# Linear attention: token turns moved from TensorE through DRAM squares to VectorE, normalisation moved to GpSimd

## What is computed

```python
# layer 0: shifted-window attention, windows of 7 x 7, 4 heads of 32
x = x + L0_conv(_gn(x), w_qkv, pos_emb, w_out, b_out)
# layer 1: tokens t = (16, 3136, 128)
t = t + L1_attn(_ln_t(t), W, b)
t = t + L1_ffn(_ln_t(t), W, V, gamma, beta)

def _ln_t(v, eps=1e-5):            # normalise each token over its channels
    m = mean(v, -1); s = var(v, -1)
    return (v - m) / sqrt(s + eps)

def L1_attn(x, W, b):              # linear attention, causal
    q, k, v = split(x @ W.T + b)
    q = elu(q) + 1; k = elu(k) + 1
    kv_cum = cumsum(k outer v); k_cum = cumsum(k)
    return (q @ kv_cum) / (q . k_cum + 1e-6)

def L1_ffn(x, W, V, gamma, beta):  # batch norm of x @ W.T over all tokens, then
    y_t = sigmoid(wx_t + y_(t-1) @ V.T)   # a recurrence over the tokens
```

## Time and profile before

| | us |
|---|---|
| median of 3 runs | 1781.64 (1780.31 to 1782.01) |
| the profiled execution | 1784.76 |
| its span | 1782.8 |

### The profile page before, as it was taken

The page is one execution under the profiler, slowest core; times in us unless marked ns, Lnnn a source line. Parts: engine busy times, 40 slices in busy tenths (PEclk is TensorE's granted clock), DMA queues, the critical chain, the costliest instruction groups (busy, mean ns, idle before and its releaser), DMA issues.

```text
span 1782.8 us, 58142 instructions
## 1 busy us (share of the span) xinstructions
PE 1749.7 (98%) x19648; PEld 1587.7 (89%) x19648; DVE 1509.8 (85%) x4546; ACT 1269.8 (71%) x3387; POOL 1073.7 (60%) x1202
## 2 busy tenths in 40 slices
PE   7999999999999999989999999999999999989997
PEld 6888888888888888879999999999999999989997
DVE  7889888888888888778888888888888888868787
ACT  5877778887887788856666666666666666657776
POOL 6887888888888888843333333333333333368874
PEclk9999999999999999999999999999999999999999
DMA  5333343433333332313334434343434443457774
GB/s 167 105 103 104 104 110 99 109 107 102 110 103 104 106 106 70 83 43 70 73 67 68 70 68 70 68 67 68 70 68 70 68 68 70 86 178 277 291 278 176
DMA packets 361816, 188.30 MB, mean 106 GB/s; under 512 B 221760, under 2 KB 348720, under 8 KB 356656
## 3 DMA queue, kind: packets, MB, share of 16 engines
q1 hardware_dynamic: 360368, 183.40, 41.0%
q10 hardware_dynamic: 1152, 1.13, 0.2%
HBM read 106.58 MB, written 77.87 MB: 103 GB/s over the span
## 4 chain that ended last, share of the span: by engine, by line
PE 52%; issue 28%; POOL 17%; DVE 1%; DMA 1%; POOLq 0%; ACT 0%; ACTq 0%; SPq 0%; DVEq 0%
POOL la_rstd L1025 12%; PE k_psum L349 7%; PE k_psum L299 6%; PE k_psum L292 6%; PE k_psum L1488 6%; PE k_psum L317 6%; PE k_psum L333 6%; PE k_psum L365 5%; PE k_psum L1478 5%; PE k_psum L283 5%; POOL la_spread L1019 3%; POOL la_tn L1030 2%; DMA wa_group<-in_group 0%; POOLq L42 0%; DMA t<-la_tn 0%
## 5 line engine op out<-in xcount | busy, mean ns | idle before, releaser
L1019 POOL TENSOR_SCALAR la_spread<-la_mv 128x4 f32<-128x4 f32 (+1 forms) x203 | 46.2, 228 | 476.1 <-DVE la_mv L1130 476.0
L618 POOL TENSOR_TENSOR wa_prob<-wa_prob,wa_peak 128x784 f32<-128x784 f32 x128 | 195.0, 1523 | 116.8 <-DVE wa_peak L484 116.8
L966 ACT ACTIVATE la_ve<-k_psum 128x256 f32<-128x256 f32 x196 | 75.6, 386 | 231.9 <-PE k_psum L847 231.9
L1025 POOL TENSOR_TENSOR la_rstd<-la_spread,k_exponent 128x4 f32<-128x4 f32 (+1 forms) x203 | 207.8, 1024 | 17.2 <-POOL la_spread L1019 0.4
L625 POOL TENSOR_TENSOR wa_prob<-wa_prob,wa_inv 128x784 f32<-128x784 f32 x128 | 195.2, 1525 | 11.3 <-DVE wa_inv L445 11.3
L835 PE MATMUL k_psum<-la_uT,la_wt 128*128 128x256 f32 x784 | 201.9, 380 | 0.0
L1085 DVE SCALAR_TENSOR_TENSOR la_fqk<-k_psum,la_raised 128x512 f32<-128x512 f32 x196 | 135.4, 691 | 72.8 <-ACT la_raised L958 72.6
L1562 ACT ACTIVATE sc_y<-k_psum,sc_cols 128x128 f32<-128x128 f32 x414 | 152.3, 368 | 51.9 <-PE k_psum L1488 8.8
L476 DVE TENSOR_TENSOR wa_prob<-k_psum,wa_bias 128x784 f32<-128x784 f32 x128 | 124.9, 976 | 66.2 <-PE k_psum L317 66.1
L1488 PE MATMUL k_psum<-sc_y,sc_vT 128*128 128x128 f32 x824 | 171.0, 289 | 0.0
L958 ACT ACTIVATE la_raised<-k_psum,la_minus_one 128x512 f32<-128x512 f32 x196 | 134.8, 688 | 43.9 <-PE k_psum L835 43.7
(11 more groups left out here) (137 smaller groups left out, 5205.3 us busy)
## 6 DMA issues: line engine op xcount, KB each, us to landing
la_xc<-x SPq DMA_DIRECT2D x196, 128.0 KB, 3.0
wa_xT<-in_x_cm SPq DMA_DIRECT2D x124, 196.0 KB, 3.3
sc_tb<-t SPq DMA_DIRECT2D x17, 1320.0 KB, 8.3
out<-sc_ob SPq DMA_DIRECT2D x17, 1280.0 KB, 5.4
wa_xw<-in_x_tok SPq DMA_DIRECT2D x64, 224.0 KB, 2.7
wa_xw<-in_x_tok SPq DMA_DIRECT2D x64, 168.0 KB, 2.3
x<-wa_y SPq DMA_DIRECT2D x64, 168.0 KB, 2.8
x<-wa_y SPq DMA_DIRECT2D x48, 224.0 KB, 2.9
```

Of the source, the lines that this page charges most:

```text
L618: nc.gpsimd.tensor_tensor(s, s, peak[:, k % S, :].unsqueeze(2).broadcast_to([128, PAIRS * HEADS, WIN]), ALU.subtract).then_inc(lowered, 1)
L1025: nc.gpsimd.tensor_tensor(rstd[:, n % S, used], spread[:, used], exponent[:, used], ALU.pow).then_inc(rooted, 1)
```

## The change

Tokens are no longer turned by TensorE. GpSimd normalises unit n (now as x * rstd + shift with shift = 1 - mean * rstd, which contains the added 1) into `u`, four pieces of 32 channels apart. When both units of a pair are there, SyncE stores the pair to a new DRAM tensor `squares` (`store_normed`, 128 partitions of 2 KB). One step later SyncE waits for that store to land and loads the pair again with four DMAs (`load_squares`), each of which puts one quarter of the channels on 32 partitions. Then VectorE turns 32 x 32 squares in `us` into `uT` with one instruction per unit (`turn_tokens`). `turned_out` on ScalarE and `turn_tokens` on TensorE are gone. Token loads run eight steps ahead (`xc` has 12 buffers), statistics and normalisation seven and six steps ahead; `steps` begin at -8, and JOIN is NU - 7. To make room, `uT` has three buffers and `raised` two.

The diff, cut to its core (signatures, semaphore lists and places where only XS becomes XC are left out):

```diff
@@ -70,0 +71 @@
+    squares = nc.dram_tensor("squares", (B * T // 512, 128, QUADS, 4 * SQ), F32, kind="Internal").ap()
...
@@ -206 +207 @@
-        JOIN = NU - 3
+        JOIN = NU - 7
...
@@ -672 +673,5 @@
-        AHEAD = 7
+        XC = 12
+        RS = 2
+        TS = 3
+        US = 2
+        AHEAD = 11
...
@@ -680 +684,0 @@
-        plus_one = sb("plus_one", [128, 1])
...
@@ -682 +686 @@
-        xc = sb("xc", [P, XS, 2, C])
+        xc = sb("xc", [P, XC, 2, C])
...
@@ -687,3 +691,5 @@
-        u = sb("u", [P, S, 2, C])
-        uT = sb("uT", [128, S, 2 * P])
-        raised = sb("raised", [128, S, 4 * P])
+        shift = sb("shift", [P, S, 2])
+        u = sb("u", [P, US, QUADS, 4, SQ])
+        us = sb("us", [128, US, QUADS, 4, SQ])
+        uT = sb("uT", [128, TS, 2 * P])
+        raised = sb("raised", [128, RS, 4 * P])
...
@@ -761 +769 @@
-        steps = range(-4, UNITS + 9)
+        steps = range(-8, UNITS + 9)
...
@@ -779,2 +787,19 @@
-                    at_least(sp, attended, n - XS + 1)
-                    sp.dma_start(xc[:, n % XS], rows(x1, n)).then_inc(loaded[n % XS], 16)
+                    at_least(sp, attended, n - XC + 1)
+                    sp.dma_start(xc[:, n % XC], rows(x1, n)).then_inc(loaded[n % XC], 16)
+
+                def store_normed(n):
+                    if not inside(n, UNITS) or n % 2 == 0:
+                        return
+                    m = n // 2
+                    sp.wait_ge(normed, n + 1)
+                    sp.dma_start(squares[m], u[:, m % US].rearrange("p q a r -> p q (a r)")).then_inc(u_stored[m % US], 16)
+
+                def load_squares(n):
+                    if not inside(n, UNITS) or n % 2 == 1:
+                        return
+                    m = n // 2
+                    sp.wait_ge(u_stored[m % US], (m // US + 1) * 16)
+                    at_least(sp, u_out, 2 * (m - US) + 2)
+                    for q in range(QUADS):
+                        sp.dma_start(us[q * SQ:(q + 1) * SQ, m % US].rearrange("p k a r -> p k (a r)"),
+                                     squares[m, :, q, :].rearrange("(k p) r -> p k r", p=SQ)).then_inc(u_loaded[m % US], 16)
...
@@ -797 +822,2 @@
-                    load(n + 4)
+                    load(n + 8)
+                    load_squares(n + 4)
...
@@ -798,0 +825 @@
+                    store_normed(n + 6)
...
@@ -817,11 +843,0 @@
-                def turn_tokens(n):
-                    if not inside(n, UNITS):
-                        return
-                    if n == 0:
-                        pe.wait_ge(*released["u"])
-                    pe.wait_ge(normed, n + 1)
-                    at_least(pe, u_out, n)
-                    for a in range(2):
-                        mm = nc.tensor.transpose(b_u[:, a * P:(a + 1) * P], u[:, n % S, a, :], ident[:, :])
-                    mm.then_inc(u_turned, 1)
-
...
@@ -832,0 +849 @@
+                    pe.wait_ge(u_out, n + 1)
...
@@ -835 +852 @@
-                        mm = nc.tensor.matmul(b_qk[:, j * 2 * P:(j + 1) * 2 * P], wt[:, j * C:(j + 1) * C], uT[:, n % S, :],
+                        mm = nc.tensor.matmul(b_qk[:, j * 2 * P:(j + 1) * 2 * P], wt[:, j * C:(j + 1) * C], uT[:, n % TS, :],
...
@@ -928 +944,0 @@
-                    turn_tokens(n + 1)
...
@@ -945,8 +960,0 @@
-                def turned_out(n):
-                    if not inside(n, UNITS):
-                        return
-                    act.wait_ge(u_turned, n + 1)
-                    at_least(act, qk_ready, n - S + 1)
-                    at_least(act, v_ready, n - S + 1)
-                    nc.scalar.activation(uT[:, n % S, :], b_u[:, 0:2 * P], ACT.Identity, bias=plus_one[:, 0:1]).then_inc(u_out, 1)
-
...
@@ -957,2 +965,2 @@
-                    at_least(act, qk_out, n - S + 1)
-                    nc.scalar.activation(raised[:, n % S, :], b_qk[:, :], ACT.Exp, bias=minus_one[:, 0:1]).then_inc(qk_raised, 1)
+                    at_least(act, qk_out, n - RS + 1)
+                    nc.scalar.activation(raised[:, n % RS, :], b_qk[:, :], ACT.Exp, bias=minus_one[:, 0:1]).then_inc(qk_raised, 1)
...
@@ -999 +1006,0 @@
-                    turned_out(n + 1)
...
@@ -1026,0 +1034,16 @@
+                    if inside(n, UNITS):
+                        pool.wait_ge(rooted, n + 1)
+                        nc.gpsimd.tensor_tensor(shift[:, n % S, :], mv[:, n % S, 0, :, 0], rstd[:, n % S, 0:2], ALU.mult).then_inc(lowered, 1)
+                        pool.wait_ge(lowered, n + 1)
+                        nc.gpsimd.tensor_scalar(shift[:, n % S, :], shift[:, n % S, :], -1.0, 1.0, ALU.mult, ALU.add).then_inc(shifted, 1)
+
+                def normalise(n):
+                    if not inside(n, UNITS):
+                        return
+                    pool.wait_ge(shifted, n + 1)
+                    at_least(pool, u_stored[n // 2 % US], n // 2 // US * 16)
+                    for a in range(2):
+                        last = nc.gpsimd.tensor_scalar(u[:, n // 2 % US, :, n % 2 * 2 + a, :], quads(xc[:, n % XC, a, :]), rstd[:, n % S, a:a + 1],
+                                                       shift[:, n % S, a:a + 1], ALU.mult, ALU.add)
+                    last.then_inc(normed, 1)
+
...
@@ -1033,2 +1056,3 @@
-                    statistics(n + 3)
-                    remember(n + 3 - AHEAD)
+                    normalise(n + 6)
+                    statistics(n + 7)
+                    remember(n + 7 - AHEAD)
...
@@ -1064 +1087 @@
-                def normalise(n):
+                def turn_tokens(n):
...
@@ -1067,10 +1090,4 @@
-                    dve.wait_ge(rooted, n + 1)
-                    at_least(dve, u_turned, n - S + 1)
-                    for a in range(2):
-                        if n < S:
-                            last = nc.vector.scalar_tensor_tensor(u[:, n % S, a, :], xc[:, n % XS, a, :], mv[:, n % S, 0, a, 0:1],
-                                                                  rstd[:, n % S, a:a + 1].broadcast_to([P, C]), ALU.subtract, ALU.mult)
-                        else:
-                            last = nc.vector.tensor_scalar(u[:, n % S, a, :], xc[:, n % XS, a, :], mv[:, n % S, 0, a, 0:1],
-                                                           rstd[:, n % S, a:a + 1], ALU.subtract, ALU.mult)
-                    last.then_inc(normed, 1)
+                    dve.wait_ge(u_loaded[n // 2 % US], (n // 2 // US + 1) * 16 * QUADS)
+                    at_least(dve, qk_ready, n - TS + 1)
+                    at_least(dve, v_ready, n - TS + 1)
+                    nc.vector.transpose(uT[:, n % TS, :], us[:, n // 2 % US, :, n % 2 * 2:n % 2 * 2 + 2].rearrange("p k a r -> p a k r")).then_inc(u_out, 1)
...
@@ -1111 +1128 @@
-                        dve.wait_ge(loaded[n % XS], (n // XS + 1) * 16)
+                        dve.wait_ge(loaded[n % XC], (n // XC + 1) * 16)
...
@@ -1126,0 +1144 @@
+                    at_least(dve, shifted, min(UNITS, n - S + 1))
...
@@ -1150 +1168 @@
-                    measure(n + 3)
+                    measure(n + 7)
...
@@ -1154,2 +1172,2 @@
-                    normalise(n + 2)
-                    aggregate(n + 3)
+                    turn_tokens(n + 2)
+                    aggregate(n + 7)
```

More of the change, by code:

```diff
@@ L85, in build @@
     with ExitStack() as ctx:
-        linear = linear_attention(nc, ctx, x1, t2, attn_wt, attn_b, masks_d, ident, ones, exponent, gram, bank,
+        linear = linear_attention(nc, ctx, x1, squares, t2, attn_wt, attn_b, masks_d, ident, ones, exponent, gram, bank,
                                   ffn, signals, (ffn_w, ffn_wt, ffn_vt, gamma, beta))
@@ L653, in _, with linear_attention @@
                 pipeline(step, **run, following=linear["gpsimd"](pool), join=JOIN + 1, prepare=(23, 24))
-def linear_attention(nc, ctx, x1, t2, attn_wt, attn_b, masks_d, ident, ones, exponent, gram, bank,
+def linear_attention(nc, ctx, x1, squares, t2, attn_wt, attn_b, masks_d, ident, ones, exponent, gram, bank,
                      ffn, signals, ffn_data):
@@ L702, in linear_attention @@
         folded = sem("la_folded")
-        loaded = [sem(f"la_loaded{i}") for i in range(XS)]
+        loaded = [sem(f"la_loaded{i}") for i in range(XC)]
+        u_stored = [sem(f"la_u_stored{i}") for i in range(US)]
+        u_loaded = [sem(f"la_u_loaded{i}") for i in range(US)]
         stored = [sem(f"la_stored{i}") for i in range(XS)]
@@ L706, in linear_attention @@
         spread_out, rooted, tabled = sem("la_spread_out"), sem("la_rooted"), sem("la_tabled")
-        normed, u_turned, u_out = sem("la_normed"), sem("la_u_turned"), sem("la_u_out")
+        lowered, shifted, normed, u_out = sem("la_lowered"), sem("la_shifted"), sem("la_normed"), sem("la_u_out")
         qk_ready, qk_raised, qk_out = sem("la_qk_ready"), sem("la_qk_raised"), sem("la_qk_out")
@@ L846, in values @@
                     for a in range(2):
-                        mm = nc.tensor.matmul(b_v[:, a * C:(a + 1) * C], uT[:, n % S, a * P:(a + 1) * P],
```

(12 more changed lines are left out.)

## The result

The changed kernel takes 2019.91 us (median of 4 runs, 2017.82 to 2023.15) where the kernel before takes 1781.83: a ratio of 1.134, 95% interval 1.1325 to 1.1352. It is 238 us slower. 44 were forecast, and the range ended at 1890. The profiled execution took 2017.8 us for a span of 2016.2.

A forecast was written before the change was run, and what follows sets the result against it. SyncE was to bound linear attention at 4.15 us per unit against 3.98 before: +32 us over 190 units, +12 on the way in, from 1784.8 to 1828.8, less 3.1: 1826 us. The range ran from 1750 to 1890.

The forecast's parts named there:

- What bounds the stage: Linear-attention stage: SyncE's round of a pair, including the landing wait, takes 8.3 us, 4.15 per unit, above TensorE's 3.76.
- The landing of the 256 KB store: SyncE's wait for the normalised pair's store to reach DRAM: 2.8 us from its issue, bounds 2.0 and 3.7.
- landings stretch: Rival: added bytes make the store's landing 3.7 us, 4.6 us per unit, 1909 us in all; chance 0.20.
- second loop: Token load, VectorE statistics, GpSimd, store landing, square loads, t2 stores: 15.5 us per four units, 3.87 per unit, not deciding.
- Other terms of SyncE's round: Per pair on SyncE: square loads 1.68 us, t2 stores 3.31, the other token load 0.43, gaps 0.08.
- The way in: Start of linear attention: SyncE waits for GpSimd's normalised pairs, delaying window output stores; three VectorE waits, +12 us (0 to 25).
- GpSimd and VectorE: Work per unit in the stage grows to 2.6 us on GpSimd and falls to 3.13 on VectorE, both below TensorE's 3.76.
- TensorE's 3.76 us per unit: In the stage TensorE loses two token turns, 0.22 us, going from 3.98 to 3.76 us per unit if nothing else is late.

The follow-up runs named there:

- e6_full: The changed kernel with t2 pieces padded to 40 floats (160 bytes), all edges on multiples of 32 bytes, three key buffers instead of four: 1872.99 us, ratio 1.0497.
- e1_swap: The changed kernel with each SyncE step's t2 stores issued ahead of the square loads and their wait: 1924.76 us, ratio 1.077.
- e10_swap_full_join: e9_swap_full with SyncE taking up linear attention at the other engines' window step, not three steps ahead: 1766.77 us, 0.9909 of the kernel before.
- e9_swap_full: e6_full with the order of e1_swap (t2 stores ahead of the square loads): 1771.33 us, 0.9935 of the kernel before.
- e12_full_shift: e6_full with the whole of t2 moved by 16 bytes, so all piece edges lie inside 32-byte blocks: 2071.08 us, ratio 1.1629.
- b6_full: The kernel before with only the t2 pieces padded as in e6_full, no new key buffers: 1782.7 us, ratio 1.0003.
- e11_start: The changed kernel with 132-byte t2 pieces at a pitch of 160, starting on multiples of 32 bytes: 1948.74 us (one run); only the stage is compared.
- e5_shift: The changed kernel with the whole of t2 moved by 16 bytes in DRAM, nothing else: 2104.09 us (one run).
- e2_late: The changed kernel with the square loads issued one step later, just ahead of the next normalised store: 1962.27 us, ratio 1.0969.

## Why the prediction was wrong in size and right in mechanism

- **What bounds the stage: right.** SyncE's landing wait stands at the head of every other wait, and the order of the round is the one summed. TensorE is busy at 79% instead of the 91 forecast, and three of four SyncE rows are nearly empty, as said.
- **The landing of the 256 KB store: the step that failed.** I took 2.8 us with bounds 2.0 and 3.7. It is 2.6 in the first stretch and 4.7 to 5.0 in the middle 147 of 196 units; the pair's round is 9.2 us in the one and 10.7 in the other (8.3 forecast). The 2.8 came from window-stage stores, whose rows are whole multiples of 32 bytes, the bound of 2.0 from the end of the kernel, and the 3.7 from the last t2 store, in the last eighth. I had the row of this stage's token loads, 3.0 us, but as a median over the whole stage. Cut by windows it would have shown 2.2 and then 3.2 us for the same transfer, a cost in this stage's own traffic that my "nearest rows" lacked. The estimate by the Trainium skill (DMA: Bandwidth & Descriptors, Anatomy of one DMA), 2.6 us, is met in the first stretch and missed by 2 us in the middle; the page gives it for DMAs that GpSimd issues, and SyncE issues these.
- **The rival "landings stretch", 1909 us:** the right direction for a wrong reason, and some 110 us short. (Its own terms add up to 1912 us; the 1909 is a slip.) I tied it to bytes; e6_full moves more bytes (121 against 100 GB/s in 1100:1200) and lands sooner. Its second loop, for four units, with 4.1 for the token load's landing and 5.0 for the store's, as e1_swap shows them, 1.8 for the t2 stores, and the prediction's other terms, comes to 18.9 us; e1_swap's four units take 19.6. But SyncE's own round in e1_swap comes as near: landing 5.0, square loads 2.0, a token load 0.5, a group of t2 stores 1.8, gaps and short waits some 0.4 us, in all 9.7 of its 9.8 us per pair. Which of the two bounds that kernel no run decides.
- **Other terms of SyncE's round:** over 1000 to 1400 us the square loads take 1.86 us (1.68 forecast), the t2 stores 1.69 per unit (1.65), a token load 0.49 (0.43). Together they are some 0.3 us per pair above the forecast, against 1.9 for the landing. The sum also left out short waits for GpSimd and VectorE and, in one step of the first stretch, the five loads of the recurrence's weights (2.4 us). So a landing of 2.8 would not have made the 4.15 us per unit true: e6_full has it in the median, and takes 4.40.
- **The way in: right.** +10 us for +12, with three waits of VectorE for output stores (18.4 us in all) where three of 5 to 6 were forecast. With those waits gone (e10_swap_full_join) the first t2 store comes 6 us sooner.
- **GpSimd and VectorE: right enough.** The two groups, 1000 to 1300 us:

```profile
L1046 POOL TENSOR_SCALAR la_u<-la_xc,la_rstd,la_shift 128x128 f32<-128x128 f32 x112 | 49.8, 452 | 0.1
L1093 DVE STREAM_TRANSPOSE la_uT<-la_us 128x256 f32<-128x256 f32 x57 | 25.4, 445 | 0.3 <-issue 0.3
```

  452 ns for 350 and 445 for 400, both inside their bounds; GpSimd's work is 2.65 us per unit (200.09 in 75.5) for 2.6, VectorE's 3.18 for 3.13. GpSimd's busy share, 50%, is below the 60 to 65 forecast only because the unit is longer.
- **TensorE's 3.76 us per unit:** not seen. With the wait nearly gone (e9_swap_full) the unit takes 3.85 at 99% busy. In the changed kernel TensorE spends 4.18 us of busy time on a unit (315.84 in 75.5) with two turns less than before, at a mean granted clock of 0.94 of 2.4 GHz, where the kernel before had 1.00: its matmuls of L852 take 409 ns each over the kernel, 380 before, which the sum put at nothing.

## What to carry to other kernels

A wait for a DMA's landing on the engine that issues all DMAs is a full term of its round; find work to issue in between, and then look at who waits for the data instead. Take the price of a landing from the stretch where it will happen, cut into windows: a median over a stage hid a step from 2.2 to 3.2 us that became 2 us per pair. And if many small pieces go to DRAM, put at least their starts on multiples of 32 bytes before anything is made to wait beside them; padding by 21% was worth 147 us here, and nothing at all where no landing was waited for.

## What was not expected of the hardware

- Pieces with both edges inside a 32-byte block lengthen the landing of *other* transfers in flight: the 256 KB store from 2.8 to 4.8 us (e6_full and e12_full_shift), the token loads, which read, from 2.1 to 3.0 (b6_full and before). With one such edge it is 2.8 us as well (e11_start). How it comes about, and why e5_shift's slow pieces are worse (6.0 us), stays open.
- The load of squares lands in 2.0 us after SyncE's wait, and in 3.4 to 3.9 right behind t2 stores (e1_swap, e2_late). With the padding it is 2.1 even there (the page of e9_swap_full).
- The mean granted clock of TensorE is lower where it stalls more: over 1000 to 1400 us it is 1.00 of 2.4 GHz at 99% busy (e9_swap_full), 0.99 at 89% (e6_full) and 0.94 at 79% (the changed kernel).
